# Relative products of causal attention: written per head in 5 KB rows, with a third staging pair

## The reference

```python
QEr = jnp.einsum('bhsd,ld->bhsl', q, Er_s)
Srel = _skew(QEr)          # row s of QEr shifted so that column t holds the product for distance s - t
QK = jnp.einsum('bhsd,bhtd->bhst', q, k)
attn = (QK + Srel) / math.sqrt(dh)
causal = jnp.tril(jnp.ones((S, S), dtype=bool))
attn = jnp.where(causal[None, None], attn, -jnp.inf)
attn = jax.nn.softmax(attn, axis=-1)
out = jnp.einsum('bhst,bhtd->bhsd', attn, v)
```

## Time and profile before

| | us |
|---|---|
| median of 3 runs | 1227.47 (1227.22 to 1229.96) |
| the profiled execution | 1220.86 |
| its span, first to last instruction | 1219.0 |
| mean granted TensorE clock | 0.933 of full speed |
| TensorE busy | 1068.6 (88% of the span) |
| VectorE busy | 661.2 (54%) |
| ScalarE busy | 635.3 (52%) |
| queue q1 of the DMA engines, share of 16 engines' span | 47.3% |

### The profile page before, as it was taken

The page is one execution under the profiler, slowest core; times in us unless marked ns, Lnnn a source line. Parts: engine busy times, 40 slices in busy tenths (PEclk is TensorE's granted clock), DMA queues, the critical chain, the costliest instruction groups (busy, mean ns, idle before and its releaser), DMA issues. The chain is left out here.

```text
span 1219.0 us, 22097 instructions
## 1 busy us (share of the span) xinstructions
PE 1068.6 (88%) x6978; PEld 665.8 (55%) x6979; DVE 661.2 (54%) x1993; ACT 635.3 (52%) x1245; POOL 199.1 (16%) x466
## 2 busy tenths in 40 slices
PE   7999999999997868999999991547999999987487
PEld 5556555555554567999999991312333333325254
DVE  4428778777776521121111102857666666774697
ACT  2457677776742422222223330516777777762797
POOL 0000000000000022122223210002222223230232
PEclk9959999999898979999999996869999999998798
DMA  5098899888966637566666654253111111100001
GB/s 181 10 302 280 281 311 293 302 272 287 295 226 225 226 118 278 190 216 216 216 216 221 230 192 147 92 184 109 49 46 48 46 45 45 47 26 9 0 32 39
DMA packets 92239, 199.56 MB, mean 164 GB/s; under 512 B 8392, under 2 KB 49608, under 8 KB 86152
## 3 DMA queue, kind: packets, MB, share of 16 engines
q1 hardware_dynamic: 88424, 188.46, 47.3%
q0 software_dynamic: 3744, 10.23, 2.2%
HBM read 134.82 MB, written 63.83 MB: 163 GB/s over the span
## 5 line engine op out<-in xcount | busy, mean ns | idle before, releaser
L775 DVE CUSTOM_DVE_ANT_0 unused<-mpsS,mask_bias 128x512 bf16<-128x512 f32 x256 | 172.1, 691 | 82.3 <-PE mpsS L708 81.9
L1516 ACT ACTIVATE hT<-ph,w 128x128 f32<-128x128 f32 x312 | 89.0, 368 | 205.1 <-PE ph L1490 186.5
L802 ACT ACTIVATE mPT<-mpsB 128x512 f32<-128x512 f32 x256 | 152.5, 597 | 80.8 <-PE mpsB L715 74.6
L1490 PE MATMUL ph<-xT,w 128*128 128x128 f32 x1248 | 151.1, 281 | 6.2 <-DMA w<-in_w1p 6.0
L1490 PEld LDWEIGHTS ph<-xT,w 128*128 128x128 f32 x1248 | 146.8, 197 | 8.6 <-issue 8.4
L1535 DVE TENSOR_TENSOR xn<-py,b 128x256 f32<-128x256 f32 x39 | 16.6, 425 | 244.9 <-PE py L1500 244.9
L1500 PE MATMUL py<-w,hT 128*128 x624 | 141.2, 379 | 0.7 <-DVE xn L1535 0.7
L650 ACT ACTIVATE scores<-scores,nm 128x512 f32<-128x512 f32 (+3 forms) x256 | 125.4, 554 | 10.5 <-DVE nm L621 10.5
L1500 PEld LDWEIGHTS py<-w,hT 128*128 128x128 f32 x624 | 115.6, 190 | 15.2 <-issue 1.1
L643 ACT COPY stage<-psE 128x1024 f32<-128x1024 f32 (+1 forms) x90 | 78.7, 874 | 83.6 <-PE psE L533 67.6
L708 PE MATMUL mpsS<-mqk 96*128 96x512 bf16 x256 | 100.5, 394 | 20.4 <-DMA mqk<-packed 17.3
(11 more groups left out here) (261 smaller groups left out, 1614.5 us busy)
## 6 DMA issues: line engine op xcount, KB each, us to landing
w<-in_w1p SPq DMA_DIRECT2D x39, 1028.0 KB, 5.6
rel<-stage SPq DMA_DIRECT2D x64, 512.0 KB, 7.5
bias<-rel SPq DMA_DIRECT2D x44, 640.0 KB, 6.0
x<-rel SPq DMA_DIRECT2D x20, 640.0 KB, 5.9
mqk<-packed SPq DMA_DIRECT2D x64, 192.0 KB
rel<-stage SPq DMA_DIRECT2D x32, 256.0 KB, 7.1
w<-in_w2p SPq DMA_DIRECT2D x8, 1024.0 KB, 12.5
b<-in_b SPq DMA_DIRECT2D x39, 128.0 KB, 5.7
```

Source lines behind the costliest of these rows:

```text
L775: nc.vector.tensor_tensor_reduce(out=unused[:, i, :], in0=psS[i % 2][:, :], in1=mask_bias[:, i, :], scale=1.0, scalar=-3.0e38, op0=ALU.add ...
L802: nc.scalar.activation(PT[r][:, j, :], psB[j % 2][:, :], ACT.Exp, scale=1.0 / 4).then_inc(s_exp, 1)
L1490: mm = nc.tensor.matmul(ph[half][:, q * P:(q + 1) * P], w1[i][:, dk * F + f * P:dk * F + (f + 1) * P], xT[i][:, dk, :], start=(dk == 0), s ...
L1516: g = nc.scalar.activation(hT[i][:, f, :], ph[half][:, q * P:(q + 1) * P], ACT.Gelu, bias=w1[i][:, DK * F + f:DK * F + f + 1])
```

## The change

The three writes of a pair, each of one unit of both heads (rows of 2, 2 and 1 KB per head), become two, each of one whole head (rows of 5 KB). `rel` becomes eight tensors of one head, each contiguous. A head's read waits for that head's write alone. SP's order becomes: the reads of pair n+4, then, when all three evictions of pair n+5 are done, its two writes. A third staging pair is added: its head 0 lies in x behind the third bias buffer, its head 1 in the tile `mask_bias`, which is otherwise used only by later stages and now is allocated early. The two heads of this third buffer lie apart, so ScalarE fills them with two copies for each unit. The tile `heads` and the weights `wkv` of the next stage now also lie in `mask_bias`.

```diff
-    rel = [dram(f"rel_{r}", (P, 2, REL_W), F32) for r in range(RING)]
+    rel = [dram(f"rel_{r}", (P, REL_W), F32) for r in range(ROUND)]
...
             REL, READ, SOFT, EXP = 5, 4, 2, 1
+            STAGES = 3
...
-                bias.append(x[:, :, :].rearrange("p t d -> p (t d)")[:, 0:2 * REL_W].rearrange("p (a w) -> p a w", a=2))
+                spare = x[:, :, :].rearrange("p t d -> p (t d)")
+                bias.append(spare[:, 0:2 * REL_W].rearrange("p (a w) -> p a w", a=2))
...
-                vals = Values(ctx, "a")
+                vals = Values(ctx, "a", wkv_flat[:, REL_W:REL_W + S])
...
-                s_wr = [[sem(f"s_wr{r}_{u}") for u in range(NU)] for r in range(RING)]
+                s_wr = [sem(f"s_wr{r}") for r in range(ROUND)]
...
+                def stage_of_head(p, h):
+                    if p % STAGES < 2:
+                        return stage[p % STAGES][:, h, :]
+                    return (spare[:, 2 * REL_W:3 * REL_W], wkv_flat[:, 0:REL_W])[h]
...
                     def read(p):
-                        for u in range(NU):
-                            sp.wait_ge(s_wr[p % RING][u], 16 * (p // RING + 1))
-                        sp.sem_inc(s_seen_sp, 1)
                         for h in range(2):
+                            slot = (2 * p + h) % ROUND
+                            sp.wait_ge(s_wr[slot], 16 * (2 * p // ROUND + 1))
+                            sp.sem_inc(s_seen_sp, 1)
                             if p >= len(bias):
                                 sp.wait_ge(s_soft, piece(p - len(bias), NU - 1, h) + 1)
-                            skewed = bass.AP(rel[p % RING].ap().tensor, P - 1 + h * REL_W, [[2 * REL_W - 1, P], [1, REL_W]])
-                            sp.dma_start(bias[p % len(bias)][:, h, :], skewed).then_inc(s_rd[(2 * p + h) % ROUND], 16)
-
-                    def write(p, u):
-                        cols = slice(512 * u, 512 * u + WU[u])
-                        sp.wait_ge(s_eev, NU * p + u + 1)
-                        if p >= RING:
-                            for h in range(2):
-                                m = 2 * (p - RING) + h
-                                sp.wait_ge(s_rd[m % ROUND], 16 * (m // ROUND + 1))
-                        sp.dma_start(rel[p % RING][:, :, cols], stage[p % 2][:, :, cols]).then_inc(s_wr[p % RING][u], 16)
+                            skewed = bass.AP(rel[slot].ap().tensor, P - 1, [[REL_W - 1, P], [1, REL_W]])
+                            sp.dma_start(bias[p % len(bias)][:, h, :], skewed).then_inc(s_rd[slot], 16)
+
+                    def write(p):
+                        sp.wait_ge(s_eev, NU * (p + 1))
+                        for h in range(2):
+                            slot = (2 * p + h) % ROUND
+                            wait(sp, s_rd[slot], 16 * (2 * p // ROUND))
+                            sp.dma_start(rel[slot][:, :], stage_of_head(p, h)).then_inc(s_wr[slot], 16)
 
                     for n in range(-REL, NP - SOFT):
-                        early, back = pair_at(n, REL), pair_at(n, READ)
-                        if early is not None:
-                            write(early, 0)
-                        if back is not None:
-                            read(back)
-                        if early is not None:
-                            write(early, 1)
-                            write(early, 2)
+                        if (p := pair_at(n, READ)) is not None:
+                            read(p)
+                        if (p := pair_at(n, REL)) is not None:
+                            write(p)
+                    for m in range(NBH - ROUND, NBH):
+                        sp.wait_ge(s_wr[m % ROUND], 16 * (m // ROUND + 1))
...
                             if early is not None:
-                                if early >= 2:
-                                    act.wait_ge(s_wr[(early - 2) % RING][u], 16 * ((early - 2) // RING + 1))
+                                cols, bank = slice(512 * u, 512 * u + WU[u]), relative_bank(early, u)
+                                if early >= STAGES and u == 0:
+                                    for h in range(2):
+                                        m = 2 * (early - STAGES) + h
+                                        act.wait_ge(s_wr[m % ROUND], 16 * (m // ROUND + 1))
                                 act.wait_ge(s_emm, NU * early + u + 1)
-                                nc.scalar.copy(stage[early % 2][:, :, 512 * u:512 * u + WU[u]],
-                                               relative_bank(early, u)[:, :, 0:WU[u]]).then_inc(s_eev, 1)
+                                if early % STAGES < 2:
+                                    nc.scalar.copy(stage[early % STAGES][:, :, cols], bank[:, :, 0:WU[u]]).then_inc(s_eev, 1)
+                                else:
+                                    nc.scalar.copy(stage_of_head(early, 0)[:, cols], bank[:, 0, 0:WU[u]])
+                                    nc.scalar.copy(stage_of_head(early, 1)[:, cols], bank[:, 1, 0:WU[u]]).then_inc(s_eev, 1)
...
-            wkv = sb(ctx, "wkv", [P, 2, DK, D])
+            mask_bias = sb(ctx, "mask_bias", [P, NI, S])
+            wkv_flat = mask_bias[:, :, :].rearrange("p i s -> p (i s)")
+            wkv = wkv_flat[:, 0:2 * DK * D].rearrange("p (n k e) -> p n k e", n=2, k=DK)
```

More of the change, by code:

```diff
@@ L363, in build, with __init__ @@
         class Values:
-            def __init__(self, ctx, tag):
+            def __init__(self, ctx, tag, heads=None):
                 self.spread = [sb(ctx, f"spread{tag}{i}", [P, GROUP, NI, CG]) for i in range(2)]
                 self.zeros = sb(ctx, f"zeros{tag}", [P, VW])
-                self.heads = sb(ctx, f"heads{tag}", [P, S])
+                self.heads = sb(ctx, f"heads{tag}", [P, S]) if heads is None else heads
                 self.rinv = sb(ctx, f"rinv{tag}", [P, 2, NI, GROUP])
@@ L957, in build @@
                     causal_attention(er, qf, identb, dmask)
-            mask_bias = sb(ctx, "mask_bias", [P, NI, S])
             maskT = sb(ctx, "maskT", [P, NI, S], BF16)
```

## The result

The changed kernel takes 1247.17 us (1244.13 to 1251.97), the one before, measured beside it, 1227.35 us; the ratio is 1.0163 with a 95% interval of 1.012 to 1.0206. The profiled execution took 1249.81 us with a span of 1248.0 us.

The account below looks back on a forecast made before the run. Transfers were taken to pace causal attention, with the engines next at 8.24 us a pair: 28 x 8.24 plus 2 for copies is 232.7 in place of 251.8, so 1227.5 - 19 = 1208.5 us; range 1201 to 1228, the forecast's own 1204 to 1213.

Parts of the forecast that it names:

- What bounds the stage: Causal attention, pairs 3 to 31: late transfers hold steps at 8.99 us; the engines alone need 8.24 us.
- the circle at SP: SP's queue: last write lands, reads issue, next writes issue and land some 7.1 us later; read issues 8.73 us apart.
- engines' floor of 8.24 us: Three attention steps without transfer waits; as the new bound, 1204 to 1213 us, chance 0.56.
- Demand: DMA engines, per pair: writes 3.4 us and reads 4.5 us, together 7.9 us, bounds 7.7 to 9.0.
- The slower rival: Write half of each circle: 5 KB writes at the reads' pace, 9.2 us a pair, 1235 us; chance 0.09.
- Order at SP: SP's queue: reads' slow start hidden under head 1's write, 0.2 us for gaps, 8.1 us a pair.
- The upper bound of the circle: SP's order, per pair: 10.0 us at most, beside the estimate of 8.1 and the engines' 8.24.
- Separate waits per head: SP's reads: head 0's waits for one 640 KB write while the other is under way; no size of its own.
- Later writes: Writes after all three evictions of a pair: latency only, 14 us at most of 16.5, nothing in the sum.
- The third pair: Staging: ScalarE's 13.8 us of waits for writes go, but overlap VectorE's and are not added.
- Split copies: ScalarE, every third pair: six copies for three, 0.47 us more; 2 us taken over ten pairs, between 0 and 4.7.
- The clock: TensorE's granted clock: the sum has it stay up without waits; a fall as now costs 4.0 us, gain 15 us.

Follow-up runs that it names:

- the order alone: Kernel before with only SP's order changed: reads of pair n+4 first, then all three writes of pair n+5; 1269.72 us, ratio 1.0374.
- head 0 first: Changed kernel, the fastest version, with SP's order write head 0 of pair n+5, reads of pair n+4, write head 1; 1205.38 us, ratio 0.9843.
- both reads together: Changed kernel with both writes of a pair awaited before either read is issued; 1273.63 us, ratio 1.0384.

## Why the prediction was wrong, step by step

*What bounds the stage*: right. Transfers paced it, the circle at SP was the form of it, and the engines' floor of 8.24 us was a good reading: 8.28 to 8.37 us came in four kernels of this study, three of which took 1205 to 1207 us, inside the 1204 to 1213 forecast for that floor. One small misreading: in the earlier trace rows the DMA engines are at 8 to 9 tenths from the third to the eleventh slice, and at 6 in the twelfth.

*Demand*: right. 3.4 us for the writes were forecast, 1.31 MB / 403 GB/s = 3.25 us were measured, 3.1 us at the 418 GB/s of the writes alone. The share of the DMA engines times the step, over pairs 3 to 31, is 0.80 x 9.93 = 7.9 us, the forecast's 7.9; before it was 0.86 x 8.99 = 7.7 us, so the faster writes don't show as a smaller demand. The slower rival, 5 KB writes at the pace of reads, is refuted, although it had the sign.

*Order at SP*: this is the step that failed. "The slow start of the reads (1.5 us long) lies under the write of head 1 ... I charge 0.2 us a circle for gaps that remain". It took the write of head 0 as landed when its bytes had moved, so that head 1's 1.6 us of bytes were still to come. In the rows after, the two writes run through one close behind the other from 208.5; from 212.0 the rate falls, and the landing of head 0 releases SP at 213.27, when little of head 1 is left; head 1's releases it about 2 us later. The next circle shows it more clearly. Its writes are issued at 215.8 and 216.2 and land 7.5 and 8.6 us later (first line), and the windows are those around the first of these landings, 223.3 us:

```profile
DMA to landing us min/median/max: 7.5/8.1/8.6
...
222.00:222.50 0.50, 0.00 (x0) 0.00 (x0) 0.50 (x1) 0.50 (x1) 0.00 (x0) 1.00 0.98 410
222.50:223.20 0.70, 0.53 (x2) 0.39 (x3) 0.70 (x3) 0.70 (x3) 0.00 (x0) 1.00 0.33 132
223.20:224.20 1.00, 1.00 (x11) 0.74 (x10) 0.97 (x3) 1.00 (x2) 0.00 (x0) 1.00 0.11 46
```

When the landing of head 0 is seen, less than two of the sixteen engines are still at work (0.11 x 16), and they move 0.05 MB in the microsecond that follows, where head 1 has 0.66 MB in all. So the cover that the prediction counted on, 1.6 us of head 1's bytes, has nearly all been moved by then. Nothing else is queued, for the order also took away what had covered this: unit 0 of the next pair, ahead of the wait. The prediction named that write as the cover ("with one small write ... to cover them"), and then didn't carry its removal into the sum. Gaps of 9.93 - 3.25 - 4.5 = 2.2 us stood in the place of 0.2 (the 4.5 us of the reads is the forecast's own; no row after measures it by itself). The upper bound of the circle, 10.0 us, came from slow writes plus the gap of now; it held the number for a wrong reason and no rival was made of it.

*Separate waits per head*: right in sign. They give back 26 of the 45 us that the order costs. That is the account of the change: 1225 us before, 1270 with the order alone, 1274 with rows and third pair but joint reads, 1247 as it is. These four times were not all taken side by side; the kernels before that stood beside them lie within 3 us.

*Later writes*: right, no cost in latency; in the version with head 0 first all evictions are awaited too, and VectorE waits for bias once in 170 us.

*The third pair*: right that ScalarE's waits go, and right not to add them; alone it is worth nothing.

*Split copies*: sized rightly and without effect. The rows after, 110 to 290 us with shapes kept apart:

```profile
L650 ACT COPY stage<-psE 128x1024 f32<-128x1024 f32 x25 | 25.3, 1013 | 23.6 <-PE psE L536 23.5
L653 ACT COPY mask_bias<-psE 128x512 f32<-128x512 f32 x12 | 7.1, 592 | 0.0
```

Two copies of 0.59 us against one of 1.013, as in the earlier trace rows. The versions with and without them (8.28 and 8.37 us a step, both with reads on GpSimd's queue) show no cost, though they differ in their rows and their staging too.

*The clock*: it went the other way. Over pairs 3 to 31 the granted clock was 0.98 before (first line) and 0.93 after (second line); from 120 to 290 us it was 1.00 in the fastest version and 0.90 in the two slowest, both reads together and the order alone:

```profile
106.55:358.36 251.81, 241.66 (x2129) 143.20 (x2124) 192.33 (x588) 173.82 (x313) 10.09 (x14) 0.98 0.86 282
...
109.00:387.00 278.00, 258.53 (x2130) 151.39 (x2124) 192.79 (x587) 175.50 (x337) 10.09 (x14) 0.93 0.80 259
```

More waits of TensorE came with more time at 1.2 GHz. That is not what makes the mean step 9.93 us, though. The trace after has two stretches with the clock at 1.00 throughout, four steps from 157.0 to 197.3 us and three from 207.8 to 238.2 us:

```profile
L624 DVE TENSOR_SCALAR nm<-mx x5: 160/161/163, 157.0 to 197.3; 128x8 f32<-128x8 f32 x5
157.03:197.30 40.27, 35.98 (x316) 21.12 (x315) 27.61 (x86) 26.10 (x49) 1.44 (x2) 1.00 0.83 260
...
L624 DVE TENSOR_SCALAR nm<-mx x4: 160/161/161, 207.8 to 238.2; 128x8 f32<-128x8 f32 x4
207.80:238.20 30.40, 27.33 (x240) 15.90 (x236) 20.37 (x64) 19.49 (x38) 0.71 (x1) 1.00 0.82 260
```

These seven steps take 10.1 us each, so the circle alone sets that pace at 2.4 GHz. Steps at a lower clock are longer, but the lead that the transfers get in them is given back: in the kernel before, two steps at 0.77 took 11.0 us each and the three behind them 8.24.

## What to carry to other kernels

When a queue waits for a transfer to land before it can issue the next one, ask what is still queued on the DMA engines during that wait; if the answer is nothing, the landing and the next start are bare in each round, and a write moved from ahead of the wait to behind it cost 45 us here. Put a large enough independent transfer ahead of the wait, or give the dependent ones a queue of their own. Each brought 1225 us down to 1205 to 1207. The second did so without larger rows or more buffers; the first was tried only with the rows of 5 KB (1210 us with two staging pairs), with 640 KB ahead of the wait where the kernel before had 512. A cover that the prediction itself names must be looked for again in the new order.

## What the runs showed of the hardware

- Two writes of 640 KB, issued 0.4 us apart, landed some 2 us apart, and the first landed 8 us after its issue, behind two reads. Through the last 1.3 us before that landing, at 213.2 us, the share of the DMA engines was 0.47 to 0.65 (a further pair, above, landed 1.5 us apart, with a share of 0.33 ahead of the first landing):

```profile
212.00:212.50 0.50, 0.00 (x0) 0.00 (x0) 0.50 (x3) 0.50 (x2) 0.00 (x0) 1.00 0.62 256
212.50:213.00 0.50, 0.40 (x1) 0.29 (x2) 0.50 (x3) 0.50 (x2) 0.00 (x0) 1.00 0.65 258
213.00:213.50 0.50, 0.50 (x4) 0.34 (x2) 0.50 (x1) 0.50 (x2) 0.00 (x0) 1.00 0.47 195
```

- Matmuls of 16 or 32 rows on different halves of the array ran at the same time, on the same rows one after the other; the difference was 1.9 us a pair (8.36 against 10.25 us a step).
- Reads issued from GpSimd's queue were as good as from SP's here (1206.4 and 1205.4 us, measured side by side). GpSimd was busy for 30.0 us from 120 to 290 us with them, against 6.5 in the changed kernel, and the time didn't suffer.
